# Eight heads' score operands made by the tensor engine in the first batch, late setup behind them, and every place of the order set anew

## The reference

```python
ga, gb = sign(ga) * max(|ga|, 0.25), sign(gb) * max(|gb|, 0.25)     # from silu(c) @ wmod, with sa, ca, sb, cb
h = layernorm(x) * (1 + ca) + sa
x = x + ga * (softmax(q k^T / 4) v @ wo + bo)                        # q, k, v = h @ w + b, 16 heads
h = layernorm(x) * (1 + cb) + sb
gate = the softmax over 16 experts, kept for the 4 largest           # router on h
x = x + gb * (2 shared experts(h) + sum of gate_e * expert_e(h))     # gelu in each
```

## Time and profile before

| | us |
|---|---|
| median of 3 runs | 959.78 |
| lowest, highest | 956.91, 961.59 |
| the profiled execution, device time | 961.51 |
| its span, first to last instruction | 959.7 |
| PE busy in it | 880.8 (92%) |
| ACT, DVE, POOL busy | 655.2, 637.9, 380.8 |

### The profile page before, as it was taken

The page is one execution under the profiler, slowest core; times in us unless marked ns, Lnnn a source line. Parts: engine busy times, 40 slices in busy tenths (PEclk is TensorE's granted clock), DMA queues, the critical chain, the costliest instruction groups (busy, mean ns, idle before and its releaser), DMA issues.

```text
span 959.7 us, 15806 instructions
## 1 busy us (share of the span) xinstructions
PE 880.8 (92%) x5928; PEld 427.1 (45%) x5928; DVE 637.9 (66%) x1239; ACT 655.2 (68%) x1109; POOL 380.8 (40%) x323
## 2 busy tenths in 40 slices
PE   5668788999999989999899998999999999998897
PEld 3222233255444444445444463445544554446565
DVE  6764776667778747877478765877577667824442
ACT  4178785677876867758687676768787767772542
POOL 4422143234525343424433344353433423455363
PEclk9759798999999999999999998999999999999999
DMA  7502301620315014230245003262014210221140
GB/s 250 175 25 93 93 1 41 181 73 2 89 44 189 1 61 121 78 107 1 61 122 159 24 24 104 69 176 88 29 39 127 107 44 2 89 100 44 47 159 23
DMA packets 48876, 78.28 MB, mean 82 GB/s; under 512 B 6680, under 2 KB 43032, under 8 KB 44704
## 3 DMA queue, kind: packets, MB, share of 16 engines
q1 hardware_dynamic: 48800, 77.27, 25.9%
HBM read 64.25 MB, written 12.86 MB: 80 GB/s over the span
## 4 chain that ended last, share of the span: by engine, by line
PE 67%; DVE 12%; ACT 9%; POOL 5%; issue 4%; DMA 2%; SPq 0%; POOLq 0%; ACTq 0%; DVEq 0%
PE scalar_bank L844 18%; PE down_bank L982 17%; PE vector_bank L912 11%; PE scalar_bank L895 6%; PE vector_bank L895 6%; DVE neg_max L801 5%; PE vector_bank L844 3%; DMA gates<-gates_by_expert 2%; DVE rows L681 2%; ACT probs L636 2%; ACT f_ring L602 2%; PE scalar_bank L924 2%; ACT q_aug L625 1%; PE vector_bank L930 1%; ACT gelu L664 1%
## 5 line engine op out<-in xcount | busy, mean ns | idle before, releaser
L801 DVE TENSOR_REDUCE neg_max<-vector_bank 128x1 f16<-128x512 f32 x479 | 306.0, 686 | 72.6 <-PE vector_bank L895 60.8
L636 ACT ACTIVATE probs<-scalar_bank 128x512 f32<-128x512 f32 x483 | 261.0, 602 | 109.9 <-PE scalar_bank L895 100.4
L586 POOL TENSOR_TENSOR act_lo<-gelu,act_hi 128x512 f16<-128x512 f32 x144 | 176.7, 1247 | 245.3 <-ACT act_hi L616 241.1
L788 DVE TENSOR_TENSOR gelu<-gelu,gates 128x512 f32<-128x512 f32 x128 | 112.5, 894 | 113.1 <-ACT gelu L664 92.2
L982 PE MATMUL down_bank<-down_hi,act_hi 128*128 128x256 f16 x576 | 160.1, 278 | 1.3 <-POOL act_lo L586 1.3
L982 PE MATMUL down_bank<-down_hi,act_lo 128*128 128x256 f16 x576 | 157.7, 274 | 0.0
L982 PE MATMUL down_bank<-down_lo,act_hi 128*128 128x256 f16 x576 | 157.7, 274 | 0.0
L664 ACT ACTIVATE gelu<-scalar_bank 128x512 f32<-128x512 f32 x144 | 84.7, 597 | 76.8 <-PE scalar_bank L844 55.5
L895 PE MATMUL scalar_bank<-q_aug,k_aug 64*128 64x512 f16 x483 | 118.7, 394 | 15.1 <-ACT gelu L664 12.6
L895 PE MATMUL vector_bank<-k_aug,q_aug 64*128 64x512 f16 x479 | 116.5, 404 | 12.8 <-ACT q_aug L625 6.0
L912 PE MATMUL vector_bank<-probs,v_aug 128*32 128x512 f32 x992 | 125.3, 628 | 0.0
(11 more groups left out here) (167 smaller groups left out, 1206.8 us busy)
## 6 DMA issues: line engine op xcount, KB each, us to landing
gates<-gates_by_expert SPq DMA_DIRECT2D x32, 1024.0 KB, 4.9
q_aug<-q_parts SPq DMA_DIRECT2D x96, 64.0 KB, 3.5
k_aug<-k_parts SPq DMA_DIRECT2D x96, 64.0 KB, 2.5
x_pre<-in_x SPq DMA_DIRECT2D x8, 512.0 KB, 4.0
x_post<-in_x SPq DMA_DIRECT2D x8, 512.0 KB, 5.1
out<-x_post SPq DMA_DIRECT2D x16, 256.0 KB, 2.5
gates<-in_w_up SPq DMA_DIRECT2D x4, 576.0 KB, 11.7
gates<-in_w_down SPq DMA_DIRECT2D x4, 576.0 KB, 4.3
```

What stands on the lines that cost most here:

```text
L586: pool.tensor_tensor(act[1][:, c, :], gelu[:, n % NGELU, :], act[0][:, c, :], ALU.subtract).then_inc(s_elo, 1)
L636: scalar.activation(probs[:, n % U, :], src[:], ACT.Exp, scale=SCALE).then_inc(taken[kind], 1)
L788: dve.tensor_tensor(g, g, gates[:, (n - NSH) % 8, :], ALU.mult).then_inc(s_gated, 1)
L801: dve.tensor_reduce(neg_max[:, (u // 2) % TT, at:at + 1], src[:], AX.X, ALU.max, negate=True).then_inc(done, 1)
```

## The change

Five things, and new numbers in all tables.

1. Batch 0's q and k of heads 0 to 7 no longer go through DRAM. ACT and DVE spread the weights of these heads, each head's 16 columns four times (`wide`, 4 copies of 128x512 each), and eight products (`first`, n = 2 * pair + w for the 4 pairs of heads, w = 0 for q and 1 for k) leave the operands already in the row layout. Two ACT passes with a scale and a shift for each row choose which rows are hi and which are full (`pick`, `shift`), and POOL's addition writes the row into `q_aug` or `k_aug`. `qk` 0 and 1, their stores and loads and `no_max` are gone for batch 0. `max` of these heads waits for `s_first` pair by pair.
2. DVE makes `ident_wide`, `pick` and, later, `shift` from the identity and the biases; PE spreads the biases by row with four small matmuls (L962).
3. The late setup is an item `late`, behind the h1T transposes and ahead of the products: PE makes modulations 1 and 2 there, and DVE its part of them, the gate modulations, the `v_aug` ones and the router weights' split.
4. POOL clears `q_aug[1]` and `k_aug[1]` instead of DVE, right behind the power step of batch 0's first layer norm.
5. `HEAD` is short and a table `EARLY` with a table `OPENING` places the rest of batch 0's start among the first maxima.

```diff
+            pool.memset(q_aug[1][:].bitcast(U32), 0).then_inc(s_aug1, 1)
+            pool.memset(k_aug[1][:].bitcast(U32), 0x3C003C00).then_inc(s_aug1, 1)
 ...
+                elif kind == "first":
+                    pair, w = divmod(n, 2)
+                    wait(pool, taken[kind], PER[kind], b, n + 1)
+                    pool.tensor_tensor((q_aug, k_aug)[w][0][:, pair, :], f_ring[:, F_RING[item][0], :], act[0][:, n % SETLEN, :],
+                                       ALU.add).then_inc(s_first, 1)
 ...
+                if m == 0:
+                    for k in range(4):
+                        scalar.activation(four_times(wide[0][:, k, :]), first_heads(w4_st[:, k, :]), ACT.Copy).then_inc(s_wide[0], 1)
 ...
+                    scalar.activation(act[0][:, n % SETLEN, :], src[:], ACT.Identity, bias=shift[:, 0, pair, w:w + 1], scale=pick[:, 4, w:w + 1])
+                    wait_f(scalar, item)
+                    scalar.activation(f_ring[:, F_RING[item][0], :], src[:], ACT.Identity, bias=shift[:, 1, pair, w:w + 1],
+                                      scale=pick[:, 5, w:w + 1]).then_inc(taken[kind], 1)
 ...
+            dve.tensor_copy(four_times(ident_wide), ident[:].rearrange("p (h d) -> p h d", d=DH).unsqueeze(2).broadcast_to([P, 8, 4, DH])
+                            ).then_inc(s_rep, 1)
+            dve.tensor_reduce(pick[:, 0:4, 0], ident[:].rearrange("p (x r d) -> p r x d", x=2, r=4), AX.XY, ALU.add).then_inc(s_pick, 1)
 ...
-            dve.memset(q_aug[1][:].bitcast(U32), 0).then_inc(s_aug1, 1)
-            dve.memset(k_aug[1][:].bitcast(U32), 0x3C003C00).then_inc(s_aug1, 1)
+                if m == 0:
+                    dve.wait_ge(s_w4s, 1)
+                    for k in range(4):
+                        dve.tensor_copy(four_times(wide[1][:, k, :]), first_heads(w4[1][:, k // DC, k % DC, :])).then_inc(s_wide[1], 1)
 ...
+                if kind == "late":
+                    pe.wait_ge(s_rep, 1)
+                    pe.wait_ge(s_small, 64)
 ...
+                    pe.wait_ge(s_mod0, 2)
+                    modulations(1)
+                    pe.wait_ge(s_pick, 9)
+                    modulations(2)
 ...
+                    if kind == "max" and b == 0 and n < 32 and n % 8 == 0:
+                        pe.wait_ge(s_first, 2 * (n // 8 + 1))
 ...
+                elif kind == "first":
+                    if n == 0:
+                        pe.wait_ge(s_wide[0], 4)
+                        pe.wait_ge(s_wide[1], 4)
+                        pe.wait_ge(s_h1lo, 2)
+                    pair, w = divmod(n, 2)
+                    split_product(dst[:], [([p[:, DC * w + c, P * pair:P * (pair + 1)] for p in wide], [p[:, c, :] for p in h1])
+                                           for c in range(DC)]).then_inc(sig, 1)
 ...
-LEAD = {"light": (12, 4, 6), "full": (0, 0, 2)}
+LEAD = {"light": (12, 0, 6), "full": (2, 0, 0), "first": (8, 6, 12)}
+HEAD = [("x_pre", 0, 1), ("h1T", 0, 0), ("h1T", 1, 0), ("late", 0, 0), ("first", 0, 0), ("first", 1, 0), ("first", 2, 0), ("first", 3, 0)]
```

More of the change, by code:

```diff
@@ L46 @@
 V_KINDS = ("max", "maxT", "oT", "wo", "v", "logit", "gateT")
-R_KINDS = ("warm", "exp", "onT", "h1T", "qk", "h2T", "up")
+R_KINDS = ("warm", "first", "exp", "onT", "h1T", "qk", "h2T", "up")
 AUG = (16 * 14, 16 * 12)
-F_KINDS = ("onT", "h1T", "qk", "h2T")
+SKIPPED = {"qk": 2}
+F_KINDS = ("first", "onT", "h1T", "qk", "h2T")
 NV, NRB = 3, 3
@@ new lines @@
+AFTER = {"max": [0, 0, 0, 0, 6.46, 6.95, 10.67, 18.38], "exp": [0, 0.39, 0.39, 0.39, 0.56, 0.77, 2.35, 3.85], "down":
+    [1.44, 8.44, 11.69, 17.88, 20.57], "up": [1.16, 2.97, 6.83, 15.66, 19.46], "gated": [6.13, 11.36, 13.81, 19.34,
+    25.51], "hi": [11.91, 14.18, 21.59, 24.96, 26.4], "turn": [25.08], "early": [16.37, 27.54, 28.58, 29.19, 29.19,
+    29.32, 29.9, 29.9], "pv": [4.79, 4.85, 11.03, 22.23], "ahead": [10.9, 14.69, 17.13, 17.38, 20.84, 20.84, 21.45,
+    25.77], "oraw": [10.47]}
@@ L164, in lead @@
 def lead(g):
-    return LEAD["light" if g + 1 < LIGHT else "full"]
+    return LEAD["first" if g == FIRST else "light" if g + 1 < LIGHT else "full"]
 def slot(g, put):
-    at = PLACES[4 if g < LIGHT else 5 if g >= NG else g % G]
+    at = PLACES[6 if g == FIRST else 4 if g < LIGHT else 5 if g >= NG else g % G]
     before = lead(g - 1) if g > FIRST else (0, 0, 0)
@@ L217, in plan @@
             g, place = MOVED.get((kind, n, b), (at + 4 * b, usual))
-            if (kind, n, b) not in HEAD and not (kind in ("x_pre", "stats1", "rows1") and b == 0):
-                put(g, place, (kind, n, b))
+            if b > 0 or kind not in ("x_pre", "stats1", "rows1", "h1T", "qk", "qk_out", "qk_in", "no_max", "v"):
+                if (kind, n, b) not in HEAD:
+                    put(g, place, (kind, n, b))
+    for (kind, n), place in EARLY.items():
+        put(FIRST, place, (kind, n, 0))
     for n, (g, place) in enumerate(SPLITS):
@@ L235, in ring @@
         values = kinds is V_KINDS and item[0] == "pv" and item[1] % TT == 0
-        if lent and item == ("max", 0, 0):
+        if lent and item == ("v", 1, 0):
             order.insert(0, banks)
@@ L357, in heads_of, with four_times, first_heads @@
             return row[:, 0:H * VW].rearrange("p (h w) -> p h w", h=H)[:, :, 1:VW]
-        def qk_part(part, n, b):
-            return act[part][:, n, :] if b == 0 and n >= 2 else qk[part][:, n % 2, :]
+        def four_times(row):
+            return row.rearrange("p (h r d) -> p h r d", r=4, d=DH)
+        def first_heads(weights):
+            return weights[:, 0:P].rearrange("p (h d) -> p h d", d=DH).unsqueeze(2).broadcast_to([P, 8, 4, DH])
         def piece(parts, n):
@@ L411, in wait_taken @@
                 elif kind != "warm":
-                    wait(eng, taken[kind], PER[kind], b, n + 1)
+                    wait(eng, taken[kind], PER[kind], b, n + 1 - SKIPPED.get(kind, 0))
         def wait_bank(eng, item):
@@ L421, in wait_f @@
                 kind, n, b = F_RING[item][1]
-                wait(eng, made_lo[kind], PER[kind], b, n + 1)
+                wait(eng, made_lo[kind], PER[kind], b, n + 1 - SKIPPED.get(kind, 0))
         @block.sync
@@ L627, in _ @@
                     ins.then_inc(taken["maxT"], 1)
-                if kind not in R_KINDS:
+                if kind not in R_KINDS or kind == "warm":
                     continue
                 src = bank(item)
-                wait(scalar, made[kind], PER[kind], b, n + 1)
+                wait(scalar, made[kind], PER[kind], b, n + 1 - SKIPPED.get(kind, 0))
                 if kind == "exp":
                     g, kc = n // U, n % U // GH
+                    if b == 0 and n == 9:
+                        scalar.wait_ge(s_setup_v, 8)
+                        scalar.wait_ge(s_gm_st, 16)
                     if n % GH == 0:
@@ L880, in _ @@
                         pe.matmul(bank(item)[:], ident16[:], w4[0][:, 0, :, :].rearrange("p c d -> p (c d)"), start=True, stop=True)
+                if kind == "late":
+                    pe.wait_ge(s_rep, 1)
+                    pe.wait_ge(s_small, 64)
+                    for pair in range(4):
+                        ins = pe.matmul(DB[1][:, 2 * pair:2 * pair + 2], ident_wide[:, P * pair:P * (pair + 1)], bqk[:, 0:4:2], start=True, stop=True)
+                    ins.then_inc(s_pickT, 1)
+                    pe.wait_ge(s_mod0, 2)
+                    modulations(1)
+                    pe.wait_ge(s_pick, 9)
+                    modulations(2)
                 if kind not in PER:
```

233 lines of the change are left out of this document (132 added, 101 removed), and 36 rows, old and new, of tables (BESIDE, MOVED).

## The result

The changed kernel takes 912.43 us (median of 4 runs, 911.08 to 913.72) where the kernel before, run beside it, takes 958.35 (4 runs, 952.96 to 961.59). The sign was right, the size was not.

A forecast was written before the change was run, and what follows sets the result against it. PE was taken as the bound, with only its idle or lower-clock time to gain; -14.2 - 3.2 - 4.9 + 1 + 4.9 = -16.4 us from 959.8 gave 943.4, stated as 943.5, range 931 to 962.

The forecast's parts named there:

- The gates' loads: Every batch's third gates load goes ahead of q's store; three DVE waits and PE stops, with their lower clock, go: -14.2 us.
- The end: Last batch: more ups and downs fill PE's two stops of 3.45 and 2.52 us around the second layer norm and router: -4.9.
- Exponentials behind `pv`: No next-group exponential stands ahead of `pv`, so ACT clears its backlog and PE's other three gelu stops go: -3.2 us.
- The start: Batch 0 up to the second group's row copies: an earlier lead is given back, +1 us, from -6 to +6.
- the modulations: At the start, modulations 1 and 2 now stand ahead of the products: 1.69 + 1.84 = 3.5 us of PE.
- DVE's rows wait for both memsets: First layer norm: POOL's two 1.80 us memsets start first and hold DVE's row operations to their end: +3.6 us.
- The rule of the Trainium skill: Two-port DVE and GpSimd operations exclude each other per instruction; DVE would enter after the first memset, losing 1.8 us, not 3.6.
- More products: At the start, eight products replace two: 36 more matmuls, 11.7 us of PE at most, in idle time before 60 us: nothing.
- New stops: All eight batches: with every place new, one new stop is allowed for, +4.9 us, from 0 to two more.
- the forecast's three gains: PE's stops removed at the gates' loads, behind `pv` and at the end: -14.2, -3.2 and -4.9, together 22.3 us.
- No rival: Rivals: start's lead carried on, 936 us (0.12); stops go, little gain, 959.5 (0.18); first gates load late, slower, 977.8 (0.13).
- The one that named the places' danger: Whole kernel: PE waits elsewhere instead, half of the 22.3 us gained, start +6, new stops 4.9: 959.5 us; chance 0.18.

The follow-up runs named there:

- old_groups_new: The kernel before with only the full groups' new places and lead from group 6 on, all places beside them old: 0.9983 of before.
- switch_price: The kernel before plus a TensorE test behind its last product, the same matmuls in blocks and mixed: one change of tile shape cost 0.106 us.
- old_beside_new: The kernel before with only the new places beside the full groups (norms, q, k, v, router, gates, outputs) from group 6 on: 1.0118 of before.
- old_joined: The kernel before with only TensorE's order changed, single downs between scores moved next to the next down: 1.0065 of before.
- new_clears_joined: The changed kernel with POOL's two clearings behind the first low parts and single downs between scores put beside the next down: 910.81 us, 0.9465 of before.
- new_clears_later: The changed kernel with POOL's two clearings moved from behind the first layer norm's power step to behind the first two low parts: 909.21 us.

## Why the prediction was wrong in size

- **The gates' loads**, -14.2: 14.8 measured alone. Right, cause and size.
- **The end**, -4.9: 3 to 8 from two sides. Right within what the runs can tell.
- **Exponentials behind `pv`**, -3.2: the stops went, the mechanism was wrong (above): taking the lead away costs 8% in the kernel before.
- **The start**, +1: between 0 and -2 in front of the new places, -4.6 in front of the old ones. Inside its bounds. Its milestones came as written for the rows (15.4, said 14.5), the first score (31.9, said 30), the row copies (69.5, said 69), DVE's gap (48.2 to 57.9 but for four short additions, said 10 us), and late for the products (25.9, said 18 to 25), the sixteenth maximum (45.7, said 43) and the exponentials (50.6, said 48). The mis-sized term is the modulations, 3.5 us from the earlier trace rows, which took 7.1: they now run where PE's matmuls still come at half speed. That DVE's rows wait for both memsets held (+3.2 measured by moving them, 3.6 said). The rule of the Trainium skill that the prediction names ("SBUF — State Buffer", section "Who interferes with whom") made it 1.8 by its letter, and this case's trace goes against that.
- **More products**, 0: the sentence "in time that is idle now" left out that the time they filled was the start's own gain. With the modulations 12.8 us were spent for 14.2.
- **New stops**, +4.9: no long one came. There is no lower clock from 200 us on and no stop over 1.1 us; new short ones did come (five for DVE's `chosen` make 5.1 us where one made 2.5), inside an idle time that fell from 32.1 to 18.3 us.
- **What was missing.** The step that failed is the first sentence: "what is to be had is the time in which PE stands still or runs at the lower clock". By it the stretch from 200 to 300 us was full at 98.75. The "rest" fell by 18.3 us with the new places and the old start. By the price 90 fewer changes of shape are 9.5 of them, and the other 9 fit the 10.8 us of short pauses; the split is worked out and not measured by itself, and old_groups_new saved 60 changes with no shorter rest. The idle time and the clock came out as forecast in size: from 200 us on they fell by 13.7 and 9.6, together 23.3, where the forecast's three gains made 22.3. A part of that is luck, since the reason of the 3.2 was wrong and short waits that the forecast didn't count went too (for ACT's `f_ring` and DVE's `neg_max`, 3.4 and 3.2 us before, 0.5 and 0.2 after). Ahead of 200 us they fell by 2.1 and 4.8 more with the same start; much of that is chance, since two executions of one and the same order up to there (before and switch_price) lost 24.5 and 19.0 us to the clock.

Against the forecast's sum, in rough numbers: +1 and +4.9 came out as about -1.5 and 0, which is 7.4 of the 29.5 us missed, and the "rest", which the forecast had at nothing, is 18.3. Some 4 us are left for what fell ahead of 200 us and for the noise. No rival came true. The one that named the places' danger (half the stops stay, new ones come) describes old_groups_new and old_beside_new well, so the danger was real: one half of the tables without the other is enough.

**Open.** Some 26 of the 47 us, those beside the gates' load and the end, belong to the new places as a whole, and no run shows which of them. Which pairs of places make the short pauses is open too: the two halves of the tables have no price one by one, and the order with the third gates' load behind the store of q wasn't tried in the changed kernel. Why the lead's removal costs the old kernel 8% is seen only in the list of its waits.

## What to carry over

Before calling an engine full, compare its instructions per stretch, not its busy share: short pauses and changes of the tile's shape both read as busy. Count changes of shape in TensorE's order (0.106 us each here) and group like with like, but only as far as the banks are free in time: of the three versions here that save changes in another way (old_groups_new, old_joined, new_clears_joined) none gained anything that can be told, and old_joined lost. When a change resets every place, price the places first; a new path at the start is worth its saved waits less the engine work that it adds.

## What the runs showed of the hardware

- A change of the tile's shape on TensorE costs 0.106 us between 128\*128 and 64\*128 and about 0.12 between 128\*128 and 128\*32 (switch_price), with no idle time shown.
- At the start the granted clock of 1.00 in a windows view is no grant. The traces hold no record of the clock before 21.37 us in the kernel before and 26.71 in the changed one, and the view counts time without a record as full. Up to there the products start 0.38 to 0.43 us apart, and from the next one on 0.217 apart: PE was at the lower level, 1.2 GHz, and rose to 2.4. The other profiled versions show the same step at their first record, or have no product ahead of it. The lines of before, with the window's 1.00, and then the changed kernel's, in which PE had been at work without a gap since 15.59:

```profile
16.00:21.00 5.00, 4.62 (x11) 1.61 (x12) 4.04 (x9) 1.26 (x2) 0.76 (x2) 1.00 0.77 295
...
21.02 0.55 PE L844 MATMUL scalar_bank<-h_hi,wqkvo_lo 128*128 128x512 f16 x1
21.41 0.38 PE L844 MATMUL scalar_bank<-h_hi,wqkvo_hi 128*128 128x512 f16 x1
21.63 0.38 PE L844 MATMUL scalar_bank<-h_lo,wqkvo_hi 128*128 128x512 f16 x1
...
26.29 0.59 PE L921 MATMUL scalar_bank<-h_lo,gelu 128*128 128x512 f16 x1
26.72 0.38 PE L921 MATMUL scalar_bank<-h_hi,act_lo 128*128 128x512 f16 x1
```

- A DVE operation that meets two memsets of POOL back to back waited for both, once more: four rows took 4.58 us in the changed kernel, and 1.38 with the memsets moved (new_clears_later).
